# Context and weights laid out by partition, and ternary weights prepared within attention

## What is computed

```python
x = x + cross_attention(layernorm(x), ctx)        # 16 heads of 32, softmax
# 32 experts x 4 sets: in every group of 32 tokens each of the 128 (expert, set)
# picks one token (argmax over tokens of x @ Wc + bc), runs a 512 -> 32 relu -> 512
# network on it, and the result is scattered back to that token
x = x + scatter(relu(gather(x_n) @ W1 + b1) @ W2 + b2)
x = x + mlstm_attention(layernorm(x), ctx)        # 8 heads of 64, gates, exp decay
def bitlinear(x, W, b):
    w_scale = clip(mean(abs(W)), 1e-5, None)
    Wq = clip(round(W / w_scale), -1, 1) * w_scale     # ternary
    xq = clip(round(x * (127 / x_scale)), -128, 127) * (x_scale / 127)
    return xq @ Wq.T + b
x = x + bitlinear(gelu(bitlinear(layernorm(x), W1, b1)), W2, b2)   # 512 -> 2048 -> 512
```

## Time and profile before

| | us |
|---|---|
| median of 3 runs | 2254.47 |
| lowest and highest | 2250.25, 2256.15 |
| the profiled execution | 2248.99 |
| its span | 2247.2 |
| PE busy in the span | 1885.3 (84%) |
| DVE, ACT, POOL busy | 1389.0, 1251.9, 629.1 |
| mean granted clock of PE | 0.907 |

### The profile page before, as it was taken

The page is one execution under the profiler, slowest core; times in us unless marked ns, Lnnn a source line. Parts: engine busy times, 40 slices in busy tenths (PEclk is TensorE's granted clock), DMA queues, the critical chain, the costliest instruction groups (busy, mean ns, idle before and its releaser), DMA issues. The chain is left out here.

```text
span 2247.2 us, 39361 instructions
## 1 busy us (share of the span) xinstructions
PE 1885.3 (84%) x14173; PEld 1145.6 (51%) x14211; DVE 1389.0 (62%) x2616; ACT 1251.9 (56%) x2311; POOL 629.1 (28%) x1139
## 2 busy tenths in 40 slices
PE   6999999999999999998577555257789889889875
PEld 3666666666666666665254322015445445445532
DVE  2757767676766757667355444124777777777763
ACT  2666656656655665666155222234776776776753
POOL 1322321322232132231000001004536336336420
PEclk9999999999999999999799766576888989989988
DMA  6433534344353433333187676767525435424200
GB/s 200 133 91 114 153 90 143 83 117 123 114 155 94 143 80 97 101 100 99 68 175 151 188 228 238 283 231 268 174 95 169 144 102 169 157 89 128 67 20 19
DMA packets 215455, 302.86 MB, mean 135 GB/s; under 512 B 62912, under 2 KB 122400, under 8 KB 207968
## 3 DMA queue, kind: packets, MB, share of 16 engines
q1 hardware_dynamic: 156656, 213.79, 30.5%
q10 hardware_dynamic: 42224, 52.97, 7.4%
q0 software_dynamic: 16384, 33.59, 5.8%
HBM read 161.60 MB, written 71.53 MB: 104 GB/s over the span
## 5 line engine op out<-in xcount | busy, mean ns | idle before, releaser
L506 DVE TENSOR_REDUCE a_negmax<-a_score 128x1 f32<-128x512 f32 x512 | 345.3, 683 | 113.1 <-PE a_score L622 105.1
L441 ACT ACTIVATE a_prob<-a_score,a_negmax 128x512 f32<-128x512 f32 x512 | 354.0, 693 | 99.0 <-DVE a_negmax L506 98.2
L317 POOL DMA_DIRECT2D a_q_stack<-a_q_parts x512 | 250.7, 498 | 517.9 <-DVE a_q_parts L500 253.9
L622 PE MATMUL a_score<-a_k_stack,a_q_stack 128*128 128x512 f32 x512 | 354.5, 693 | 10.0 <-ACT a_prob L441 8.3
L630 PEld LDWEIGHTS a_turn<-a_ident,a_prob 128*128 128x128 f32 x2048 | 253.9, 141 | 134.6 <-issue 93.5
L630 PE MATMUL a_turn<-a_ident,a_prob 128*128 128x128 f32 x2048 | 308.8, 274 | 3.4 <-ACT a_perm L417 2.0
L325 DVE COPY a_probT<-a_turn 128x512 f32<-128x512 f32 x256 | 176.2, 688 | 213.5 <-PE a_turn L630 213.3
L325 ACT COPY a_probT<-a_turn 128x512 f32<-128x512 f32 x256 | 150.3, 587 | 280.3 <-PE a_turn L630 278.7
L2001 PE MATMUL c_ff<-c_w2T,c_hqT 128*128 128x512 bf16 x482 | 144.1, 459 | 40.1 <-ACT c_hqT L1537 34.3
L622 PEld LDWEIGHTS a_score<-a_k_stack,a_q_stack 128*128 128x128 f32 x512 | 97.4, 190 | 112.8 <-issue 74.8
L651 PE MATMUL a_mix<-a_probT,a_v 128*32 128x128 f32 x4096 | 138.9, 276 | 0.1
(11 more groups left out here) (210 smaller groups left out, 3335.3 us busy)
## 6 DMA issues: line engine op xcount, KB each, us to landing
a_k_stack<-a_k_parts SPq DMA_DIRECT2D x512, 64.0 KB, 2.6
a_q_stack<-a_q_parts POOLq DMA_DIRECT2D x512, 64.0 KB, 2.3
scratch_res<-b_chosen SPq DMA_DIRECT2D x32, 1024.0 KB, 4.7
c_res<-scratch_res SPq DMA_DIRECT2D x32, 1024.0 KB, 7.6
c_hid<-in_L_ffn_W ACTq DMA_DIRECT2D x16, 1024.0 KB, 7.1
c_negm<-scratch_m SPq DMA_DIRECT2D x64, 256.0 KB, 4.4
a_xs<-in_x ACTq DMA_DIRECT2D x8, 1024.0 KB, 5.4
scratch_cT<-a_cT SPq DMA_DIRECT2D x8, 1024.0 KB, 5.2
```

Of the source, the lines that this page charges most:

```text
L317: eng.dma_start(stack[kind][i * DH0:(i + 1) * DH0, M % 2, g, :].bitcast(F32), parts[kind][g * DH0:(g + 1) * DH0, part, :].bitcast(F32)).th ...
L441: nc.scalar.activation(prob[:, U % 4, :], score.bank(U)[:, :], ACT.Exp, bias=negmax[:, u:u + 1], accum_out=sums[:, head_of(U), tile_of(U): ...
L506: nc.vector.tensor_reduce(negmax[:, U % UNITS:U % UNITS + 1], score.bank(U)[:, :], AX.X, ALU.max, negate=True).then_inc(max_ready, 1)
L622: nc.tensor.matmul(score.bank(U)[:, :], stack["Q"][:, M % 2, g, t * P:(t + 1) * P], stack["K"][:, M % 2, g, :], start=True, stop=True).the ...
```

## The change

The host lays out five inputs anew, without arithmetic on them: the context turned per batch (128 partitions, 4 blocks, 512 tokens), W1 of the experts with 4 KB per partition and group, W2 of the experts as 128 rows of 512 (already turned), their first bias turned, and the ternary part's two matrices as 8 pieces of 128x2048 in the order in which PE wants them.

- Attention has no `cs`, no CT turns, no ACT copies of them and no store of `cT`; the context goes straight to one of two `cT` buffers. SP loads the first two, ACT issues the load of batch b+2 at u = 26, after the last K product. The routing weights and the normed result stand in natural feature order.
- The 512 steps are cut into 16 pieces of 32. In pieces 0 to 7 ACT sums absolute values in four parts of 128x512 at steps 8, 12, 16, 20 of the piece. In pieces 8 to 15 ACT scales at these steps, DVE clips a step later, ACT rounds to bf16 another step later and issues a store of 128 KB one step later still. The next MB is loaded at step 24. The two scales are made with one matmul at u = 58 of batch 3.
- The experts' phase has W2 in six buffers, loaded by SP, no sort, no turn, no copy of it; W1 by one transfer per group; 6 banks for the gather's ring.
- In the tail SUM, TOTAL, WSCALE, QUANT, CLIP, W and WCOPY are gone; the rest of the lists stays as it is. LOADW is now two loads of 2 MB of bf16 from scratch, issued after the first norm, and the context is read from the input.

```diff
-             (17, "R", 0, 0), (25, "CT", 0, 1), (27, "CT", 1, 1), (29, "CT", 2, 1), (31, "CT", 3, 1),
+    PIECE_UNITS, PIECE_AT, PIECE_STEP = ALL // (2 * PIECES), 8, 4
...
+                def sum_weights(w, k):
+                    if k == 0:
+                        act.wait_ge(weights_in, 16 * (w + 1))
+                    nc.scalar.activation(weights[:, k, :], weights[:, k, :], ACT.Abs,
+                                         accum_out=w_sums[:, 4 * w + k:4 * w + k + 1]).then_inc(w_summed, 1)
...
+                def round_weights(w, k):
+                    n = w - PIECES
+                    if 4 * n + k > 0:
+                        act.wait_ge(w_stored, 16 * (4 * n + k))
+                    act.wait_ge(w_clipped, 4 * n + k + 1)
+                    nc.scalar.activation(rounded[:, :], weights[:, k, :], ACT.Identity, bias=down[:, :]).then_inc(w_rounded, 1)
+                def store_weights(w, k):
+                    n = w - PIECES
+                    act.wait_ge(w_rounded, 4 * n + k + 1)
+                    act.dma_start(scratch["W"][n, :, k * 512:(k + 1) * 512], rounded[:, :]).then_inc(w_stored, 16)
...
+                        if rest == 0:
+                            (sum_weights if piece < PIECES else scale_weights)(piece, k)
...
+                        work.wait_full(act, 0, jobs["K", b, GROUPS - 1])
+                        act.dma_start(cT[:, b % 2], A["ctx_T"][b + 2]).then_inc(c_in[b % 2], 16)
...
+                def clip_weights(w, k):
+                    dve.wait_ge(w_scaled, 4 * (w - PIECES) + k + 1)
...
-    NW, NR = 4, 4
+    NW, NR, N2 = 4, 4, 6
...
-        work = Ring(ctx, sems, nc, "b_work", 4, 4)
+        work = Ring(ctx, sems, nc, "b_work", 6, 6)
...
-                    for r in ROWS:
-                        sp.dma_start(w1[r, q % NW].rearrange("p e c f -> p e (c f)"),
-                                     w1_d[j, r, :, h * CH * F:(h + 1) * CH * F]).then_inc(w1_in[q % NW], 16)
+                    sp.dma_start(w1[:, q % NW].rearrange("p e c f -> p (e c f)"), A["experts_W1"][h, j]).then_inc(w1_in[q % NW], 16)
+                def load_w2(e):
+                    sp.dma_start(w2[:, e % N2, :], A["experts_W2"][e]).then_inc(w2_in[e % N2], 16)
...
                     sp.dma_start(res_d[e], results(e)).then_inc(res_stored[e % NR], 16)
+                    if e + N2 < EXP:
+                        load_w2(e + N2)
...
-                        for w in range(NH):
-                            load_weight(w)
+                        act.dma_start(w1T[:, :, :], scratch["W"][0:C].rearrange("c p n -> p c n")).then_inc(w_in, 16)
+                        act.dma_start(w2T[:, :, :].rearrange("p (r k) d -> p r (k d)", r=C),
+                                      scratch["W"][C:2 * C].rearrange("r p n -> p r n")).then_inc(w_in, 16)
```

More of the change, by code:

```diff
@@ L371, in _ @@
                                allow_small_or_imprecise_dtypes=True).then_inc(tie_ready, 1)
+                for tile, fill in ((one, 1.0), (up, ROUND), (down, -ROUND)):
+                    nc.gpsimd.memset(tile[:, :], fill).then_inc(pool_const, 1)
                 stack_parts(pool, "Q", 0)
@@ L659, in turn_tiles @@
                     cols = slice(n * P, (n + 1) * P)
-                    if kind == "CT" and n == 0:
-                        pe.wait_ge(c_in, b * 16 + 16)
-                    elif kind == "XT" and n == 0:
+                    if kind == "SUM":
+                        turn.wait_free(pe, 0, j)
+                        pe.wait_ge(w_total, 1)
+                        nc.tensor.matmul(turn.bank(j)[:, 0:2], one[:, :].to_broadcast([P, P]), w_sum[:, :],
+                                         start=True, stop=True).then_inc(turn.full[j % 2], 1)
+                        return
+                    if kind == "XT" and n == 0:
                         pe.wait_ge(xn_ready, b + 1)
@@ L841, in _ @@
                     load_tokens(1, b)
+                for e in range(N2):
+                    load_w2(e)
                 for e in range(EXP):
@@ L906, in first_layer @@
                     last.then_inc(aux.full[q % 2], 1)
-                def turn_w2(e):
-                    pe.wait_ge(w2_sorted, e + 1)
-                    wt.wait_free(pe, 0, e)
-                    for c in range(C):
-                        last = nc.tensor.transpose(wt.bank(e)[:, c * P:(c + 1) * P], w2s[:, e % 2, c, :], ident[:, :])
-                    last.then_inc(wt.full[e % 2], 1)
                 def second_layer(e):
@@ L2002, in down @@
                     last.then_inc(ff.full[j % 3], 1)
-                def turn_weight(n):
-                    pe.wait_ge(w_taken, n + 1)
-                    for k in range(W_JOBS):
-                        transposes(ff, job["W", 0, n] + k, lambda i: low(piece(PIECES + n)[:, (PACK * k + i) * P:(PACK * k + i + 1) * P]), bf=True)
-                def total():
-                    j = job["TOTAL", 0, 0]
-                    ff.wait_free(pe, 0, j)
-                    pe.wait_ge(w_total, 1)
-                    nc.tensor.matmul(ff.bank(j)[:, 0:2], one[:, :].to_broadcast([P, P]), w_sum[:, :],
-                                     start=True, stop=True).then_inc(ff.full[j % 3], 1)
                 for kind, m, n in items(PE_ORDER):
```

357 lines of the change are left out of this document (147 added, 210 removed), and 11 rows, old and new, of the table PE_ORDER.

## The result

The changed kernel takes **2128.9 us** (median, 2128.4 to 2136.7) against 2254.1 for the kernel before (four executions each): a ratio of **0.9462** (95% interval 0.9446 to 0.9478). The forecast was 2133.7, range 2103 to 2170. The profiled execution has a span of 2126.6 us against 2247.2, 120.6 less; the sum had said 120.8. That the total fits so well is partly luck: single stages are off by up to 4 us, either way.

A forecast was written before the change was run, and what follows sets the result against it. It took PE to bound attention, a chain or latency the second layer, and transfers the last phase's start. Its terms summed to -120.8 us, taking the 2254.5 us median to 2133.7, range 2103 to 2170.

The forecast's parts named there:

- Second layer: Experts' second layer: mostly DMA-bound at 3.45 us per expert instead of 5.8, saving 73 us (59 to 81).
- Rival 1: Second layer: PE's chain at its slow clock binds, 3.9 us per expert, -59, total 2148; 0.2 together with rival 4.
- rival 4: Second layer: mixed reads and writes run at 365 GB/s, not 404; 115 us instead of 104, total 2145; 0.2 with rival 1.
- The insertions' 8: Attention: the ternary weight work put on ACT and DVE, 79 us if fully exposed, costs 8 us (-3 to +40).
- rival 2: Attention: inserted ACT work about half exposed, +40 instead of +8, total 2166 (2205 if fully exposed); chance 0.14.
- rival 5: All cover holds: no loss in attention, 3.25 us per expert in the second layer, total 2119; chance 0.15.
- The turns' 12: Attention loop: 28 groups of context transposes leave PE at 0.44 us each, saving 12 us.
- The prologue's 7.5: Attention's prologue: Q's product starts at about 21.3 us instead of 28.9, saving 7.5 us (4 to 9).
- 5.8 + 2.5: Experts' first layer: 5.8 us from no late W1 loads; then 2.5 (0 to 3.5) from PE's wait for ACT.
- Start of the tail: Last phase: index table 20.5 us earlier (12 to 22), loads of x, m, g 3.5, ACT's weight copies 4.
- Rival 3: Attention: roundings wait for the previous tile's store, 138 us lost, slower than before at 2264; chance 0.02.
- Rival 6: Second layer: W1 loads or stores, not W2, held it, so 5.8 us per expert stays, total 2207; chance 0.04.

The follow-up runs named there:

- half: Changed kernel with experts' stores of 0.5 MB rather than 1 MB, the last phase reading that half twice in split loads; 2149.7 us, ratio 0.955.
- ring4: Changed kernel with four banks rather than six for the gather's products and the second layer; 2140.4 us, ratio 0.9517.
- at2: Changed kernel with the weight work of each 32-step piece in attention starting at step 2 instead of 8; 2128.8 us, ratio 0.9456.
- double: Changed kernel with each of the 96 inserted ACT operations preceded by an in-place copy of the same 128x512 tile; 2146.7 us, ratio 0.955.
- ctturns: Changed kernel without attention's inserted ACT and DVE work and 1 MB loads, with 28 groups of four PE turns and ACT copies put back; 2135.7 us, ratio 0.9501.
- w1runs: Changed kernel with the experts' W1 in runs of 256 bytes and two transfers of 64 partitions per group; 2142.7 us, ratio 0.9521.
- loadfirst: Changed kernel with the two 2 MB ternary weight loads issued first in the last phase, not after the first norm; 2139.2 us, ratio 0.9507.

## Why the prediction was right, point by point

**What bounds the kernel.** The three stages named by the windows (PE in attention, a chain or a latency in the second layer, transfers at the start of the last phase) are where the time went: 10.7, 75.6 and 20.0 of 120.6 us.

**The signs.** The first K product came at 9.9 us (10 to 11 forecast), the first Q product at 24.4 (21). Waits for exponentials stayed under 50 us, at 49. The stores stand 3.21 us apart at a share near 1 (3.4 to 3.5 forecast). The index table was to land within 5 us of its issue and took 8.1; it still came 11.7 us after the phase's first issue, where I had 11.2, since it was issued earlier.

**Second layer.** Right, and for the reason given: DMA is the bound. 3.21 us per expert are nearly the 3.25 that 42 MB at 404 GB/s gave, and not the 3.45 that I took. 31 experts give 99.4 us instead of 107. Of these 7.6 us a term that I had mis-sized took back 4.5: from the last store's issue to the next phase's first issue, 4.7 of landing and 2.4 of change in my sum, it is 11.6 us. My sum also starts the stage at 1247 where the first store is at 1248.69; from there it gives 71.9, not 73, and at 3.25 per expert 78, not 81. Rival 1 (PE at its lower clock binds) did not come about, though the clock was low: 0.71 from 1240 to 1320. half shows 2.92 us per expert with DMA out of the way. But rival 1 was not far. My two prices for the chain, 2.5 us at the full clock and 3.9 at half of it, give by a straight line in the time of a clock cycle 2.9 at half's 0.79, as measured, and 3.1 at the changed kernel's 0.71, an estimate: 0.1 us under what DMA takes. With four banks (ring4) the chain does bind, at 3.72 us and a clock of 0.69 in the same window, where my prices give 3.1; the other 0.6 is what four banks cost, by this estimate. The sentence of the prediction that doesn't hold for this stage is "six banks instead of four change none of its links: nothing". It is true of the gather, of which it was said, and I had not asked it of the second layer; that the six banks were there is why the sum came out.

The trace settles the other rule, too. The Trainium skill ("DMA: Bandwidth & Descriptors", section "Where 436 GB/s comes from") has the HBM side bind at about 358 GB/s between HBM and SBUF. It stood beside rival 4, which rested on the 365 of a window of loads. The trace does not agree: 416 GB/s over 80 us of stores with some loads, which are nearer to the 435 that the same section gives for the SBUF side. One core works in this program; no run here has a second one loading beside it.

**Attention.** The sum 12 - 8 + 7.5 = 11.5 met 10.7. That is luck in part: the prologue gave 3 less than forecast and the loop 2 more, and one trace of attention scatters by 5. The insertions' 8 is about 6 in the traces, and at most a few us in the times. Moving them to other steps (at2) changed nothing. That they would get dearer the more there are is shown by double. So rival 2 (about half exposed, 40 us) is out, and of rival 5 (all cover holds) the part on the second layer is true and the part on attention is not, by 6 us. The turns' 12 lies between the 8.3 and 15.9 of ctturns. The prologue's 7.5 was 3 too much: I followed the context and the weights to PE, and not the biases that ACT waits for ahead of its copies.

**Experts before the second layer.** 5.8 + 2.5 met 4.3 + 2.7. Another 2.3 and 2.9 us came in the two gathers, which I had at nothing. w1runs gives back the 2.6 of pass 1, so these belong to W1; the 1.2 of pass 0 are within the scatter, and that part stays open. W1's layout and cut are worth 13 us by the ratios (6 to 21 with their intervals), a third of it in the second layer.

**Start of the tail.** The table: 20.5 met 20.0. Of the further 7.5 only 3.7 came. The load of x took 8.1 us before and after, so my estimate that the loads behind the table ran slowly beside the weight loads was wrong for the one that counts. From x's landing to the first up product it is 3.8 us less, near the 4 that I had for ACT's copies; no run takes these copies alone. From the phase's first issue to the first up product it is 23.7 us less (172.1 to 148.4), where I had 28. The rest of the ternary work in ACT, 30 us, shows no gain in that stretch, so it was covered, as I had said.

**Rival 3** (slower by waits for the store of rounded tiles) did not show: in the list of waits of attention ACT never waits for such a store. **Rival 6** is excluded by the period itself, 3.21 with the same stores.

## What to carry to other kernels

Work moved from a stage with a hand-over chain into another engine's idle time is cheap in its first dose (here 55 us of ACT's busy time for about 6) and a third exposed in its next, so measure the second dose before a third is added. When a wait is removed from a chain that runs beside a DMA stream, work out the stream's time per item from bytes and the best rate in the trace, and then ask of every ring and buffer in the new chain, banks included, whether it lets the stream be the bound. After a transfer is moved away, follow what now arrives last (a 2 KB bias, the x issued behind a scatter): two small changes of order gave 12 us more.

## What the runs showed of the hardware that I had not expected

- 416 GB/s for 80 us of stores of 1 MB mixed with loads of 256 KB, at a DMA share of 1.02.
- The engine that issues pays while DMA is full: the issue of a store rises from 0.33 to as much as 1.46 us in the second layer, and those of two small tables from 0.40 and 0.62 to 6.14 and 5.18 us in loadfirst, with 4 MB under way that another engine had issued.
- A load of 256 KB issued on SP's queue behind three and ahead of seven loads of 1 MB on ACT's took 24.86 us to land in the kernel before, and 8.1 us where these loads were gone.
- The loads of experts' results cut into two of 64 partitions that read the same bytes (half): a median of 7.7 us to landing for each half instead of 6.8, and 24 us more from the first up product to the end (664.9 against 640.8; 633.9 to 644.5 in the other kernels). What of it the cut costs is not shown.
